# Output stage of an attention block on one Trainium2 core: scale, limit and old-stream add moved to VectorE in groups, column 0 and statistics at the end

## The chip, the cores and the metric

The kernel runs on one core of a Trainium2 chip. The metric is the device time of one execution in microseconds (us), from start to end of the program on the chip. The engines of the core that matter here are TensorE (PE in the profile, with its weight loads as PEld), VectorE (DVE), ScalarE (ACT), GpSimd (POOL) and SyncE (SP), which issues transfers (DMA). Each engine works through its own instructions in order; they meet at semaphores.

## The reference, cut to what matters

The program is two transformer layers on a stream of 4096 tokens by 256 columns. The part that the change touches is the end of the second layer's attention: the output projection, an exponential map at the point (1, 0, ..., 0), a limit, a new column 0, and the residual add; after it comes the layer norm of the mixture of experts.

```
def _project(x):
    sp = jnp.clip(x[..., 1:], -8.0, 8.0)
    x0 = jnp.sqrt(1.0 + jnp.sum(sp ** 2, axis=-1, keepdims=True) + EPS)
    return jnp.concatenate([x0, sp], axis=-1)
def _exp_map(x, v):
    vx = _inner(v, x)[..., None]
    v_tan = v + vx * x
    v_ns = jnp.maximum(_inner(v_tan, v_tan), 0.0)
    v_n = jnp.minimum(jnp.sqrt(v_ns + EPS)[..., None], 5.0)
    res = jnp.cosh(v_n) * x + jnp.sinh(v_n) * v_tan / (v_n + EPS)
    return _project(res)
...
    return _project(_exp_map(mu, out @ Wo.T))
...
x = x + _L1_attn_ref(_layernorm(x, axis=-1), ...)
x = x + _L1_ffn_ref(_layernorm(x, axis=-1), ...)
```

With mu = (1, 0, ..., 0) every token's columns 1 to 255 are multiplied by one number, sinh(v_n) / (v_n + EPS), and limited to -8 and 8; column 0 becomes the square root of 1 plus the sum of the 255 squares. Then the old stream is added, and mean and variance of each token are wanted.

## The kernel before, in words

The stream lies in the on-chip memory as `u` (the tile `wide_x` in the profile): 128 partitions, 32 token tiles `t` (NT) of 256 columns. The function `attention_out` is one stage, closed by a barrier of all engines. It runs in four phases, and each engine's order is the order in which the code is written.

1. Projection (L1792 to L1821 and L1867 to L1883). TensorE turns and multiplies, VectorE copies the product into `u` two tiles at a time, ScalarE squares each tile for v_n.
2. One small chain on tiles of 128x32 (L1824 to L1846), mostly on VectorE, with a square root and two exponentials on ScalarE. It ends in `g`, one factor for each token.
3. The loop over eight groups `n` of G = 4 tiles. ScalarE multiplies each tile by its column of `g` (`scale`, L1895), four instructions of 128x256 for a group, one group ahead. VectorE limits the group in one instruction of 128x1024 (L1851). ScalarE then squares each tile with an accumulated sum into `s2` (L1904); in the trace a square is an ACTIVATE and an ACTIVATION_READ_ACCUMULATOR.
4. When all 32 sums are there: VectorE adds 1 (L1853), ScalarE loads its table for the square root and takes it (L1907), VectorE writes column 0 (L1856), and then, group by group, adds the old stream `x2` (`ao_x`, 128x1024, L1861) and takes the statistics of the four tiles (`bn_stats`, L1864).

SyncE loads the old stream: groups 0 to 3 into a ring of four places at the start of the stage, then the weights of four experts (`meanwhile`, L1915 to L1918), then groups 4 to 7, each when the add of the group four before it is done. That wait is on the semaphore `added`, which the add on VectorE raises (L1861).

After the stage comes `route`: VectorE merges the statistics (`bn_aggr`, L323) and normalises the tiles (L335) for the router on TensorE and ScalarE. The first layer has a stage much like this one, `combine_and_log_map`, whose rows serve below: there VectorE normalises a tile with two per-partition operands (L1206), limits a group (L1209), and at the end multiplies tiles by one per-partition factor `lm_f` (L1236), while GpSimd adds pairs of rows (L1272).

Of the kernel before, what the change touches and what calls it, by code (L numbers as in the profile page):

```python
# [14 lines left out]
ALU = mybir.AluOpType  # L15
ACT = mybir.ActivationFunctionType
# [7 lines left out]
P = 128  # L24
T, C = 4096, 256
KC = C // P
NT = T // P
# [1731 lines left out]
def attention_out(nc, k, meanwhile):  # L1759
# [6 lines left out]
    G = 4  # L1766
    u = k.x
    NG, NPR, XR = NT // G, NT // 2, 4
    with Stage(nc, "ao") as s:
        x2 = s.sb("x2", [P, XR, G, C])  # L1770
        oT = s.sb("oT", [P, 2, KC, 2, P])
        junk = s.sb("junk", [P, C])
        s2, vn, e1, e2, t2, pl, sm, g = (s.sb(v, [P, NT]) for v in ("s2", "vn", "e1", "e2", "t2", "pl", "sm", "g"))
        psT = s.ps("psT", [P, 2, BANK])
        psU = s.ps("psU", [P, 3, 2 * C])
        (turned, oT_out, u_ready, u_out, squared, chain, asked, done_act, scaled, clipped, led, added) = (
# [3 lines left out]
        with nc.Block() as block:  # L1780
# [35 lines left out]
            @block.vector  # L1816
            def _(dve):
                ser = Serial(dve, chain)
                for n in range(NPR):
                    dve.wait_ge(u_ready, n + 1)  # L1820
                    dve.tensor_copy(u[:, 2 * n:2 * n + 2, :],  # L1821
                                    psU[:, n % 3, :].rearrange("p (t c) -> p t c", c=C)).then_inc(u_out, 1)
                dve.wait_ge(squared, NT)
                ser(dve.tensor_scalar(vn[:, :], s2[:, :], 0.0, EPS, ALU.max, ALU.add))  # L1824
                dve.sem_inc(asked, 1)
                dve.wait_ge(done_act, 1)
                ser(dve.tensor_scalar(vn[:, :], vn[:, :], 5.0, None, ALU.min))
                dve.sem_inc(asked, 1)

                ser(dve.tensor_tensor(t2[:, :], vn[:, :], vn[:, :], ALU.mult))  # L1830
                ser(dve.tensor_scalar(pl[:, :], t2[:, :], 1.0 / 42.0, 1.0, ALU.mult, ALU.add))
                ser(dve.scalar_tensor_tensor(pl[:, :], t2[:, :], 1.0 / 20.0, pl[:, :], ALU.mult, ALU.mult))
                ser(dve.tensor_scalar(pl[:, :], pl[:, :], 1.0, None, ALU.add))
                ser(dve.scalar_tensor_tensor(pl[:, :], t2[:, :], 1.0 / 6.0, pl[:, :], ALU.mult, ALU.mult))
                ser(dve.tensor_scalar(pl[:, :], pl[:, :], 1.0, None, ALU.add))
                ser(dve.tensor_tensor(pl[:, :], pl[:, :], vn[:, :], ALU.mult))
                ser(dve.tensor_scalar(sm[:, :], vn[:, :], 0.5, None, ALU.is_lt))
                dve.wait_ge(done_act, 3)
                ser(dve.tensor_tensor(e1[:, :], e1[:, :], e2[:, :], ALU.subtract))
                ser(dve.tensor_scalar(e1[:, :], e1[:, :], 0.5, None, ALU.mult))  # L1840
                ser(dve.tensor_tensor(pl[:, :], pl[:, :], e1[:, :], ALU.subtract))
                ser(dve.tensor_tensor(pl[:, :], pl[:, :], sm[:, :], ALU.mult))
                ser(dve.tensor_tensor(e1[:, :], e1[:, :], pl[:, :], ALU.add))
                ser(dve.tensor_scalar(t2[:, :], vn[:, :], EPS, None, ALU.add))
                ser(dve.reciprocal(e2[:, :], t2[:, :]))
                ser(dve.tensor_tensor(g[:, :], e1[:, :], e2[:, :], ALU.mult))  # L1846
                dve.sem_inc(asked, 1)
                for n in range(NG):
                    part = u[:, n * G:(n + 1) * G, :]
                    dve.wait_ge(scaled, (n + 1) * G)  # L1850
                    dve.tensor_scalar(part, part, -8.0, 8.0, ALU.max, ALU.min).then_inc(clipped, 1)  # L1851
                dve.wait_ge(squared, 2 * NT)
                ser(dve.tensor_scalar(s2[:, :], s2[:, :], 1.0, EPS, ALU.add, ALU.add))  # L1853
                dve.sem_inc(asked, 1)
                dve.wait_ge(done_act, 4)
                dve.tensor_copy(u[:, :, 0], s2[:, :]).then_inc(led, 1)  # L1856
                dve.wait_ge(led, 1)
                for n in range(NG):
                    part = u[:, n * G:(n + 1) * G, :]
                    dve.wait_ge(x2_in[n % XR], (n // XR + 1) * 16)  # L1860
                    dve.tensor_tensor(part, part, x2[:, n % XR, :, :], ALU.add).then_inc(added, 1)  # L1861
                    dve.wait_ge(added, n + 1)
                    for t in range(n * G, (n + 1) * G):
                        dve.bn_stats(k.st6[:, t, :], u[:, t, :])  # L1864

            @block.scalar
            def _(act):  # L1867
                for n in range(NPR + 1):
                    if n < NPR:
                        act.wait_ge(turned, n + 1)  # L1870
                        if n >= 2:

                            act.wait_ge(u_ready, n - 1)
                        act.activation(oT[:, n % 2, :, :, :].rearrange("p k q c -> p (k q c)"), psT[:, n % 2, :],
                                       ACT.Copy).then_inc(oT_out, 1)
                    if n:
                        m = n - 1
                        act.wait_ge(u_out, m + 1)
                        for q in range(2):
                            if m or q:  # L1880

                                act.wait_ge(squared, 2 * m + q)
                            act.activation(junk[:, 1:C], u[:, 2 * m + q, 1:C], ACT.Square,  # L1883
                                           accum_out=s2[:, 2 * m + q:2 * m + q + 1]).then_inc(squared, 1)
                act.wait_ge(asked, 1)
                act.activation(vn[:, :], vn[:, :], ACT.Sqrt).then_inc(done_act, 1)
                act.wait_ge(asked, 2)
                act.activation(e1[:, :], vn[:, :], ACT.Exp).then_inc(done_act, 1)
                act.activation(e2[:, :], vn[:, :], ACT.Exp, scale=-1.0).then_inc(done_act, 1)
                act.wait_ge(asked, 3)  # L1890
                act.wait_ge(u_out, NPR)

                def scale(n):
                    for t in range(n * G, (n + 1) * G):
                        act.activation(u[:, t, :], u[:, t, :], ACT.Copy, scale=g[:, t:t + 1]).then_inc(scaled, 1)  # L1895

                scale(0)
                for n in range(NG):
                    if n + 1 < NG:
                        scale(n + 1)  # L1900
                    act.wait_ge(clipped, n + 1)
                    for t in range(n * G, (n + 1) * G):
                        act.wait_ge(squared, NT + t)
                        act.activation(junk[:, 1:C], u[:, t, 1:C], ACT.Square,  # L1904
                                       accum_out=s2[:, t:t + 1]).then_inc(squared, 1)
                act.wait_ge(asked, 4)
                act.activation(s2[:, :], s2[:, :], ACT.Sqrt).then_inc(done_act, 1)  # L1907


# [290 lines left out]
```

## Time and profile before

| | |
|---|---|
| median of 3 runs | 2615.57 us (2615.17 to 2617.49) |
| the profiled execution: its own time | 2617.34 us |
| its span from first to last instruction | 2615.5 us |
| mean granted TensorE clock | 0.935 |
| VectorE busy | 1267.7 us (48%) |
| ScalarE busy | 1490.9 us (57%) |
| small chain ready (`g`) | 1849.25 us into the span |
| last statistics of the stage | 1900.98 us into the span |

The profiled execution is a run of its own, 1.8 us above the median. Busy shares are means over the whole program; the stage of the change is 2% of it, and what it costs is read from its own stretch, 1849 to 1902 us.

### The profile page before, as it was taken

The numbers are of one execution on the slowest core, as the hardware profiler recorded it, in microseconds if no ns is written. First come the engines' busy times: TensorE is split into PE (matmuls) and PEld (weight loads), VectorE is DVE, ScalarE is ACT, GpSimd is POOL, SyncE is SP. The second block draws the span as 40 slices with busy tenths as digits, with TensorE's granted clock in tenths as the row PEclk, the third lists the DMA queues.
The fourth block names the chain that finished last, engine by engine and source line by source line (L and its number), as shares of the span: only waits on it lengthen the run. The fifth ranks groups of instructions, "written<-read, shape, count | busy, mean of one in ns | idle before, by whom it ended". The sixth has DMA issues, their size and how long they took to land. (4 is left out here: it accounts for less than half of the span.)

```text
span 2615.5 us, 41239 instructions
## 1 busy us (share of the span) xinstructions
PE 2241.7 (86%) x12824; PEld 1058.3 (40%) x12825; DVE 1267.7 (48%) x2731; ACT 1490.9 (57%) x2463; POOL 383.2 (15%) x628
## 2 busy tenths in 40 slices
PE   4995799922978999999999999999157999999993
PEld 3783555511651222222222222224124666666662
DVE  5566422254885444444444444421465444444444
ACT  2212433213766999999999999997643222222220
POOL 0030366640000000000000000000001222222220
PEclk9998899965998999999999999999678999999996
DMA  5001122253100000000000000003353444434445
GB/s 179 1 1 65 33 79 78 74 187 124 36 14 1 1 1 1 1 1 1 1 1 1 1 1 1 1 1 102 93 169 103 122 121 118 120 118 118 120 116 210
DMA packets 106610, 164.39 MB, mean 63 GB/s; under 512 B 9592, under 2 KB 82032, under 8 KB 106480
## 3 DMA queue, kind: packets, MB, share of 16 engines
q1 hardware_dynamic: 91696, 121.24, 15.1%
q0 software_dynamic: 13632, 37.24, 4.3%
q10 hardware_dynamic: 1152, 4.19, 0.4%
q8 instruction: 79, 1.29, 0.2%
q14 instruction: 51, 0.42, 0.0%
HBM read 123.06 MB, written 39.58 MB: 62 GB/s over the span
## 5 line engine op out<-in xcount | busy, mean ns | idle before, releaser
L1661 ACT ACTIVATE at_pexp<-at_psS 128x1024 f32<-128x1024 f32 x1024 | 968.1, 1023 | 59.9 <-PE at_psS L1561 56.9
L1675 DVE TENSOR_REDUCE at_mx<-at_psM 128x1 f32<-128x512 f32 x474 | 327.5, 691 | 478.4 <-PE at_psM L1588 478.4
L1575 PE MATMUL at_psO<-at_pexp,at_vst 128*32 128x512 f32 x4096 | 546.5, 606 | 0.1
L1561 PE MATMUL at_psS<-l1c_QT,l1c_KT 64*128 64x512 f16 x2048 | 404.3, 387 | 12.2 <-ACT at_pexp L1661 6.1
L1561 PEld LDWEIGHTS at_psS<-l1c_QT,l1c_KT 64*128 64x128 f16 x2048 | 100.7, 93 | 616.7 <-ACT at_pexp L1661 555.7
L1988 PE MATMUL ex_psH<-wide_wgu,ex_xT 128*128 x852 | 339.7, 549 | 0.1
L2032 ACT ACTIVATE ex_sg<-ex_bias 128x228 f32<-128x228 f32 x213 | 83.7, 393 | 287.9 <-DVE ex_bias L2058 287.9
L2058 DVE TENSOR_TENSOR ex_bias<-ex_psH,ex_bias 128x456 f32<-128x456 f32 x213 | 134.7, 633 | 198.5 <-PE ex_psH L1988 197.3
L1988 PEld LDWEIGHTS ex_psH<-wide_wgu,ex_xT 128*128 128x128 f32 x852 | 157.4, 191 | 138.1 <-issue 138.0
L1005 POOL DMA_INDIRECT expert_rows<-ex_y,ex_odx x142 | 140.4, 989 | 397.8 <-issue 281.4
L2011 PE MATMUL ex_psY<-wide_w2b,ex_hT 114*128 (+1 forms) x852 | 196.0, 380 | 0.7 <-DVE ex_y L2077 0.7
L1588 PE MATMUL at_psM<-at_ksumT,l1c_QT 64*128 64x512 bf16 x474 | 179.2, 378 | 0.6
L2011 PEld LDWEIGHTS ex_psY<-wide_w2b,ex_hT 114*128 114x128 f32 (+1 forms) x852 | 156.5, 190 | 19.6 <-issue 1.3
L999 POOL DMA_INDIRECT ex_xg<-normed,ex_idx x142 | 139.6, 983 | 112.0 <-POOL ex_odx L990 97.6
L1055 PE MATMUL ex_psH<-l_w,ex_xT 128*128 x284 | 141.9, 623 | 5.3 <-issue 1.1
L1537 POOL COPY at_vst<-wide_x 128x512 f32<-128x512 f32 x16 | 9.7, 608 | 898.7 <-PE at_psO L1575 898.6
L1575 PEld LDWEIGHTS at_psO<-at_pexp,at_vst 128*32 128x32 f32 x4096 | 80.9, 108 | 130.1 <-issue 121.6
L266 PE MATMUL w_ps<-top_ident,w_raw 128*128 128x128 f32 x128 | 23.3, 333 | 116.3 <-DMA w_raw<-in_L_attn_Wq 90.6
L1116 DVE TENSOR_SCALAR ex_y<-ex_psY,top_wgt 128x256 f32<-128x256 f32 x71 | 34.3, 484 | 176.8 <-DMA expert_rows<-ex_y,ex_odx 94.9
L2024 ACT ACTIVATE ex_xT<-ex_psX 128x256 f32<-128x256 f32 x71 | 27.2, 383 | 157.5 <-PE ex_psX L1977 157.5
L1093 ACT ACTIVATE ex_hT<-ex_psG 128x256 f32<-128x256 f32 x71 | 27.2, 383 | 132.1 <-PE ex_psG L1064 132.1
L985 POOL CAST ex_idx<-top_tok 128x1 uint32 (+1 forms) x142 | 28.6, 201 | 427.4 <-POOLq L74 304.1
(335 smaller groups left out, 2696.0 us busy)
## 6 DMA issues: line engine op xcount, KB each, us to landing
ex_bias<-in_L_ffn_bg SPq DMA_DIRECT2D x71, 342.0 KB, 4.7
ex_bias<-in_L_ffn_b SPq DMA_DIRECT2D x71, 342.0 KB, 5.1
normed<-rt_area SPq DMA_DIRECT2D x16, 512.0 KB, 2.6
lm_y<-expert_rows SPq DMA_DIRECT2D x16, 512.0 KB
cb_y<-expert_rows SPq DMA_DIRECT2D x16, 512.0 KB, 9.6
w_raw<-in_L_ffn_w SPq DMA_DIRECT2D x24, 256.0 KB, 4.2
wide_wgu<-in_L_ffn_Wg SPq DMA_DIRECT2D x8, 684.0 KB
wide_wgu<-in_L_ffn_W SPq DMA_DIRECT2D x8, 684.0 KB
```

The costliest lines, as they stand in the source:

```text
L999: pool.indirect_dma_start(xg[:, g, :], None, k.xn_d, bass.IndirectOffsetOnAxis(idx[:, g, :], 0)).then_inc(got[g], 16)
L1005: pool.indirect_dma_start(k.y_d, bass.IndirectOffsetOnAxis(odx[:, j, :], 0), y[:, j, :], None).then_inc(put[j], 16)
L1055: mm = pe.matmul(psH[:, j, :], xT[:, j, kk, :], k.w13[:, ds(e, 1), kk, :].rearrange("p a c -> p (a c)"), start=(kk == 0), stop=(kk == KC - 1))
L1561: mm = pe.matmul(psS[:, n, hh * BANK:(hh + 1) * BANK], keys(k.KT, p)[r, kt * P:(kt + 1) * P], keys(k.QT, p)[r, c * BANK:(c + 1) * BANK], s ...
L1575: mm = pe.matmul(psO[g * VW:(g + 1) * VW, y, :], vst[:, p % 2, hh, kt, :], pexp[:, (p * ST + step) % 3 * 2 + n, hh * BANK:(hh + 1) * BANK] ...
L1588: pe.matmul(psM[:, :], keys(k.QT, p)[r, t * P:(t + 1) * P], ksumT[r, p % 2, :], start=True, stop=True).then_inc(maxed, 1)
L1661: act.activation(pexp[:, u % 6, :], psS[:, u % 2, :], ACT.Exp, scale=D ** -0.5 / (QS * QS)).then_inc(raised, 1)
L1675: dve.tensor_reduce(mx[:, n:n + 1], psM[:, :], AX.X, ALU.max).then_inc(reduced, 1)
L1988: mm = pe.matmul(psH[:, n, 0:G2].rearrange("p (n c) -> p n c", n=2), xT[:, j, kk, :], k.wgu[:, ds(e, 1), kk, :, n * HW:(n + 1) * HW].rearr ...
L2011: mm = pe.matmul(psY[:, 0:C], hT[0:rows, j, g, :], k.w2b[0:rows, ds(e, 1), g, :].rearrange("p a c -> p (a c)"), start=(g == 0), stop=(g == ...
L2032: act.activation(sg[:, n, :], bias[:, st.slot(1, BR), n, 0, :], ACT.Silu).then_inc(gated, 1)
L2058: dve.tensor_tensor(hb, psH[:, n, 0:G2].rearrange("p (n c) -> p n c", n=2), hb, ALU.add).then_inc(added, 1)
```

## The change

VectorE takes over the multiplication by `g`, which also does the lower limit (L1852 of the changed kernel); the group's instruction of 128x1024 does the upper limit alone (L1855). The add of the old stream for columns 1 to 255 moves into the same loop, one group behind (L1862), and a copy of the old stream's column 0 goes to a small tile `x0` first (L1860), because the ring place is given back by the add. ScalarE keeps only the squares. Column 0 is written once, as root plus `x0` (L1868), after the last add, and the 32 statistics follow it in one run (L1871).

```
+        x0 = s.sb("x0", [P, NT])
...
-                dve.sem_inc(asked, 1)
-                for n in range(NG):
-                    part = u[:, n * G:(n + 1) * G, :]
-                    dve.wait_ge(scaled, (n + 1) * G)
-                    dve.tensor_scalar(part, part, -8.0, 8.0, ALU.max, ALU.min).then_inc(clipped, 1)
+                for n in range(NG + 1):
+                    if n < NG:
+                        part = u[:, n * G:(n + 1) * G, :]
+                        for t in range(n * G, (n + 1) * G):
+                            dve.tensor_scalar(u[:, t, :], u[:, t, :], g[:, t:t + 1], -8.0, ALU.mult,
+                                              ALU.max).then_inc(scaled, 1)
+                        dve.wait_ge(scaled, (n + 1) * G)
+                        dve.tensor_scalar(part, part, 8.0, None, ALU.min).then_inc(clipped, 1)
+                    if n:
+                        m = n - 1
+                        part = u[:, m * G:(m + 1) * G, 1:C]
+                        dve.wait_ge(x2_in[m % XR], (m // XR + 1) * 16)
+                        dve.tensor_copy(x0[:, m * G:(m + 1) * G], x2[:, m % XR, :, 0])
+                        dve.wait_ge(squared, NT + (m + 1) * G)
+                        dve.tensor_tensor(part, part, x2[:, m % XR, :, 1:C], ALU.add).then_inc(added, 1)
                 dve.wait_ge(squared, 2 * NT)
                 ser(dve.tensor_scalar(s2[:, :], s2[:, :], 1.0, EPS, ALU.add, ALU.add))
                 dve.sem_inc(asked, 1)
                 dve.wait_ge(done_act, 4)
-                dve.tensor_copy(u[:, :, 0], s2[:, :]).then_inc(led, 1)
+                dve.wait_ge(added, NG)
+                dve.tensor_tensor(u[:, :, 0], s2[:, :], x0[:, :], ALU.add).then_inc(led, 1)
                 dve.wait_ge(led, 1)
-                for n in range(NG):
-                    part = u[:, n * G:(n + 1) * G, :]
-                    dve.wait_ge(x2_in[n % XR], (n // XR + 1) * 16)
-                    dve.tensor_tensor(part, part, x2[:, n % XR, :, :], ALU.add).then_inc(added, 1)
-                    dve.wait_ge(added, n + 1)
-                    for t in range(n * G, (n + 1) * G):
-                        dve.bn_stats(k.st6[:, t, :], u[:, t, :])
+                for t in range(NT):
+                    dve.bn_stats(k.st6[:, t, :], u[:, t, :])
...
-                act.wait_ge(asked, 3)
-                act.wait_ge(u_out, NPR)
-
-                def scale(n):
-                    for t in range(n * G, (n + 1) * G):
-                        act.activation(u[:, t, :], u[:, t, :], ACT.Copy, scale=g[:, t:t + 1]).then_inc(scaled, 1)
-
-                scale(0)
                 for n in range(NG):
-                    if n + 1 < NG:
-                        scale(n + 1)
                     act.wait_ge(clipped, n + 1)
                     for t in range(n * G, (n + 1) * G):
                         act.wait_ge(squared, NT + t)
                         act.activation(junk[:, 1:C], u[:, t, 1:C], ACT.Square,
                                        accum_out=s2[:, t:t + 1]).then_inc(squared, 1)
-                act.wait_ge(asked, 4)
+                act.wait_ge(asked, 3)
                 act.activation(s2[:, :], s2[:, :], ACT.Sqrt).then_inc(done_act, 1)
```

VectorE from the end of the small chain (`ao_g` is `g`, `ao_s` is `s2`, `top_st` the statistics), before the change: all eight limits, then the tail, of which the first two groups stand here.

```order
L1846 TENSOR_TENSOR ao_g<-ao_e 128x32
L1851 TENSOR_SCALAR wide_x<-wide_x 128x1024 x8
L1853 TENSOR_SCALAR ao_s<-ao_s 128x32
L1856 COPY wide_x<-ao_s 128x32
L1861 TENSOR_TENSOR wide_x<-wide_x,ao_x 128x1024
L1864 BN_STATS top_st<-wide_x 128x6 x4
L1861 TENSOR_TENSOR wide_x<-wide_x,ao_x 128x1024
```

The same place after the change, up to the limit of group 2 (the copy L1860 reads the old stream and writes `x0`, and both are named `ao_x` there).

```order
L1847 TENSOR_TENSOR ao_g<-ao_e 128x32
L1852 TENSOR_SCALAR wide_x<-wide_x,ao_g 128x256 x4
L1855 TENSOR_SCALAR wide_x<-wide_x 128x1024
L1852 TENSOR_SCALAR wide_x<-wide_x,ao_g 128x256 x4
L1855 TENSOR_SCALAR wide_x<-wide_x 128x1024
L1860 COPY ao_x<-ao_x 128x4
L1862 TENSOR_TENSOR wide_x<-wide_x,ao_x 128x4x255
L1852 TENSOR_SCALAR wide_x<-wide_x,ao_g 128x256 x4
L1855 TENSOR_SCALAR wide_x<-wide_x 128x1024
```

Each group's four multiplications stand ahead of its limit, and the add of a group stands behind the limit of the next one. The end of the stage on VectorE after the change:

```order
L1855 TENSOR_SCALAR wide_x<-wide_x 128x1024
L1860 COPY ao_x<-ao_x 128x4
L1862 TENSOR_TENSOR wide_x<-wide_x,ao_x 128x4x255
L1860 COPY ao_x<-ao_x 128x4
L1862 TENSOR_TENSOR wide_x<-wide_x,ao_x 128x4x255
L1864 TENSOR_SCALAR ao_s<-ao_s 128x32
L1868 TENSOR_TENSOR wide_x<-ao_s,ao_x 128x32
L1871 BN_STATS top_st<-wide_x 128x6 x32
```

No add of the old stream is left behind the root; only the 32 statistics are. ScalarE before the change, from the exponentials on:

```order
L1888 ACTIVATE ao_e<-ao_vn 128x32
L1889 ACTIVATE ao_e<-ao_vn 128x32
L1895 ACTIVATE wide_x<-wide_x,ao_g 128x256 x8
L1904 ACTIVATE ao_junk,ao_s<-wide_x 128x255 x4
L1895 ACTIVATE wide_x<-wide_x,ao_g 128x256 x4
```

And ScalarE after the change, from the same place to the end of the stage:

```order
L1895 ACTIVATE ao_e<-ao_vn 128x32
L1896 ACTIVATE ao_e<-ao_vn 128x32
L1901 ACTIVATE ao_junk,ao_s<-wide_x 128x255 x32
L1904 ACT_TABLE_LOAD
L1904 ACTIVATE ao_s<-ao_s 128x32
```

The 32 multiplications are gone from ScalarE, no table load has come between the exponentials and the squares, and the one for the square root stands directly behind the last square, as before.

## Rows read from the trace of the kernel before

**Rows 1.** The page: busy time, share of the span and instructions of each engine
```profile
PE 2241.7 (86%) x12824; PEld 1058.3 (40%) x12825; DVE 1267.7 (48%) x2731; ACT 1490.9 (57%) x2463; POOL 383.2 (15%) x628
```
**Rows 2.** Busy time by stretch (busy us and instructions of each engine; TensorE clock; DMA share)
```profile
1849.30:1878.50 29.20, 0.00 (x0) 0.00 (x0) 5.55 (x8) 28.31 (x96) 0.00 (x0) 0.50 0.06 21
1878.50:1901.00 22.50, 0.00 (x0) 0.00 (x0) 20.73 (x42) 1.55 (x3) 0.00 (x0) 0.50 0.32 94
```
**Rows 3.** Who waited for whom, 1843 to 1925 us: us in total, times, longest
```profile
PE rt_psT L790 <- DVE rt_area L335: 63.5, 1, 63.5
DVE wide_x L1851 <- ACT wide_x L1895: 20.2, 8, 2.9
DVE top_mv L323 <- PEq L74: 0.8, 1, 0.8
```
**Rows 4.** Timeline of ScalarE, the group loop: start, us, what
```profile
1849.34 3.30 ACT L1895 ACTIVATE wide_x<-wide_x,ao_g 128x256 f32<-128x256 f32 x8 [2.47 <-DVEq L1847]
...
1854.57 1.69 ACT L1895 ACTIVATE wide_x<-wide_x,ao_g 128x256 f32<-128x256 f32 x4
1856.16 0.40 ACT L1904 ACTIVATE ao_junk<-wide_x 128x255 f32<-128x255 f32 x1
...
1858.08 0.19 ACT L1904 ACTIVATION_READ_ACCUMULATOR ao_junk<-wide_x 128x1 f32 x1
1858.18 1.69 ACT L1895 ACTIVATE wide_x<-wide_x,ao_g 128x256 f32<-128x256 f32 x4
...
1878.35 0.19 ACT L1904 ACTIVATION_READ_ACCUMULATOR ao_junk<-wide_x 128x1 f32 x1
1878.56 1.28 ACT L1907 ACT_TABLE_LOAD   x1
1879.85 0.23 ACT L1907 ACTIVATE ao_s<-ao_s 128x32 f32<-128x32 f32 x1
```
**Rows 5.** Timeline of VectorE, from `g` to the barrier
```profile
1849.06 0.19 DVE L1846 TENSOR_TENSOR ao_g<-ao_e 128x32 f32<-128x32 f32 x1
...
1878.57 0.18 DVE L1853 TENSOR_SCALAR ao_s<-ao_s 128x32 f32<-128x32 f32 x1 [3.54 <-ACT ao_junk L1904]
1880.11 0.20 DVE L1856 COPY wide_x<-ao_s 128x32 f32<-128x32 f32 x1 [1.36 <-ACT ao_s L1907]
1880.35 1.23 DVE L1861 TENSOR_TENSOR wide_x<-wide_x,ao_x 128x1024 f32<-128x1024 f32 x1
1881.61 1.40 DVE L1864 BATCH_NORM_STATS2 top_st<-wide_x 128x6 f32<-128x256 f32 x4
1882.93 1.21 DVE L1861 TENSOR_TENSOR wide_x<-wide_x,ao_x 128x1024 f32<-128x1024 f32 x1
...
1899.57 1.41 DVE L1864 BATCH_NORM_STATS2 top_st<-wide_x 128x6 f32<-128x256 f32 x4
```
**Rows 6.** VectorE's groups by form: busy us, mean ns of one, idle before
```profile
L1861 DVE TENSOR_TENSOR wide_x<-wide_x,ao_x 128x1024 f32<-128x1024 f32 x8 | 9.7, 1210 | 0.0
L1851 DVE TENSOR_SCALAR wide_x<-wide_x 128x1024 f32<-128x1024 f32 x8 | 5.6, 694 | 20.2 <-ACT wide_x L1895 20.2
L1236 DVE TENSOR_SCALAR lm_sp<-lm_sp,lm_f 128x256 f32<-128x256 f32 x16 | 4.3, 346 | 0.1
L2167 DVE TENSOR_SCALAR l1w_wqkv<-l1w_wqkv 128x1024 f32<-128x1024 f32 x1 | 0.7, 695 | 0.9 <-PEq L74 0.9
L877 DVE TENSOR_SCALAR rt_mask<-rt_one 128x256 f32<-128x256 f32 x2 | 0.6, 294 | 0.1
```
**Rows 7.** Timeline of VectorE in the first layer's like stage
```profile
566.53 2.35 DVE L1199 TENSOR_SCALAR lm_std<-top_mv 128x4 f32<-128x4 f32 x1
...
615.62 4.29 DVE L1236 TENSOR_SCALAR lm_sp<-lm_sp,lm_f 128x256 f32<-128x256 f32 x16
```
**Rows 8.** GpSimd at that first place, and the spread of L1199
```profile
566.51 2.34 POOL L1272 TENSOR_TENSOR lm_y<-lm_y 128x1024 f32<-128x1024 f32 x1 [3.07 <-DMA lm_y<-expert_rows]
...
L1199 DVE TENSOR_SCALAR lm_std<-top_mv x8: 169/446/2352, 560.9 to 603.8; 128x4 f32<-128x4 f32 x8
```
**Rows 9.** Loads of the old stream: landing, and the last four on SyncE
```profile
DMA to landing us min/median/max: 3.5/3.7/7.3
...
1881.60 8.01 SPq L1790 DMA_DIRECT2D ao_x<-stream  x4
```
**Rows 10.** Busy time by stretch, around the end of the weight loads (columns as rows 2)
```profile
1852.00:1854.00 2.00, 0.00 (x0) 0.00 (x0) 0.69 (x1) 1.94 (x8) 0.00 (x0) 0.50 0.35 116
1854.00:1856.00 2.00, 0.00 (x0) 0.00 (x0) 0.00 (x0) 1.97 (x8) 0.00 (x0) 0.50 0.02 7
```

## The prediction

> **What bounds the kernel now.** The page's busy shares come first: TensorE leads with 86% [rows 1], but that is a mean over a program of many stages, so they only say that no engine has an answer for this one. The page's chain covers the last 35 us alone. So I read the stage by stretches of time. From 1849.3 to 1878.5 us ScalarE is busy 28.31 of 29.20 us and VectorE 5.55; from 1878.5 to 1901 VectorE is busy 20.73 of 22.50 and ScalarE 1.55; TensorE and GpSimd do nothing in either [rows 2]. Two engines thus work one after the other. The waits say the same: VectorE's eight limits wait 20.2 us for ScalarE's multiplications, and TensorE's next work waits 63.5 us, ended by VectorE's first normalised tile [rows 3]. Everything after the stage hangs on VectorE's last statistics, so a microsecond off the path from `g` to there should be a microsecond off the program.
>
> The timeline of ScalarE shows its price for a group: four multiplications and four squares, 3.61 us from one group to the next (1854.57 to 1858.18) [rows 4]; 32 multiplications and 32 squares make 1849.34 to 1878.54. That of VectorE shows the tail: from 1880.35 to 1900.98, eight times 2.57 us for an add and four statistics [rows 5].
>
> **The change, part by part.** I lay the new instructions out in time from rows, and measure the new end against the old one, 1900.98.
>
> *Prices.* A multiplication by a per-partition factor on a tile of 128x256 in on-chip memory is L1236: 346 ns for one [rows 6], and 16 in a row take 4.29 us [rows 7], so the next starts (4.29 - 0.346) / 15 = 0.263 us after the one before. The new one adds a constant lower limit to it. With constants alone that shape takes 294 ns [rows 6], and a limit with two constants on 128x1024 takes 694, so a second operation is not what costs. Four: 3 x 0.263 + 0.346 = 1.14 us. The upper limit is an instruction of the old form: 0.69, and 0.04 before it, since it waits for the four (gaps of this kind, 0.03 to 0.04, stand between an instruction and one that waits for it, as from 1880.31 to 1880.35 [rows 5]). An instruction behind one that it does not wait for starts 0.08 before that one's end (1881.61 + 1.40 is 1883.01, the next starts at 1882.93 [rows 5]). The copy of 128x4 has no row: the nearest, L1199, has the same size and takes 0.17 at the least and 2.35 beside GpSimd [rows 7, 8]. GpSimd is idle here, so I take 0.17, overlapped at both ends, 0.08 of the path, and keep 0.17 as its upper bound. The add on 4x255 columns reads 1020 elements instead of 1024: 1.21 [rows 6].
>
> *A group on VectorE:* 1.14 + 0.04 + 0.69 - 0.08 + 0.08 + 1.21 - 0.08 = 3.00 us. *A group on ScalarE:* the squares alone, 1856.16 to 1858.27, 2.11 us [rows 4]. So the pace passes from ScalarE (3.61) to VectorE (3.00), and ScalarE waits 0.9 us in each group.
>
> *In time.* `g` is there at 1849.25 [rows 5]. Group 0 is multiplied 1849.29 to 1850.43 and limited by 1851.16; group 1 is limited by 1852.95. ScalarE squares group 0 from 1851.19 to 1853.30, so the first add waits 0.4 us and ends at 1854.54. This is the one place where the add waits for squares: from then on an add starts 3.00 us behind its group's limit and the squares need 2.14. Group 2 starts at 1854.46, group 7 five periods later at 1869.46, limited by 1871.33. Its squares end at 1873.47, while VectorE is through with the add of group 6 at 1872.54 and waits 0.96 us. The last add runs 1873.50 to 1874.71.
>
> *The tail.* ScalarE's table load needs no semaphore: it stood 0.02 us behind the last square before [rows 4], so it runs 1873.47 to 1874.75, under the last add, and about 1.3 us of it leave the path. `s2` plus 1 ends at 1874.81, the root (0.23) at 1875.07, column 0 (0.20) at 1875.30. The statistics start at 1875.34. Four take 1.40 where one takes 0.41 (L1864 spaced 0.33), so 32 take 31 x 0.33 + 0.41 = 10.6 us: the end is 1885.95, 15.0 us before the old one. By parts: 29.2 us of loop become 24.2, and 22.4 us behind the last square become 12.5, and the difference there is the eight adds, 1.24 each with its gap: seven now lie under the squares, and the last lies over the table load, in whose place it stands.
>
> The table load is where a page is weighed. The row has 1.28 us of load and the root 0.01 behind it, so the root waits for 1.28 only [rows 4]. The Trainium skill, page "ScalarE: Activation LUTs", section "What ACT_TABLE_LOAD costs", says that a switch costs about 2.66 us, the load and a drain of 1.38 with it. By that estimate the root would end 1.3 us later and the gain be 13.7; the trace does not agree with it, and the sum goes by the row.
>
> *What is moved past queues.* SyncE's loads of groups 4 to 7 wait for the adds. They were issued from 1881.60 [rows 9] and now could be from 1854.6, one each 3 us. The weight loads ahead of them have drained: the transfer share is 0.35 up to 1854 and 0.02 after [rows 10]. The load for group 4 has from 1854.6 to 1865.3, 10.8 us, and the slowest of the eight landed in 7.3 [rows 9]: hidden. If that cover went, each us of landing beyond 10.8 would be a us on the path. Behind the add on VectorE the next group's multiplications are queued, and ScalarE's squares wait for those. The barrier's 0.8 us [rows 3] stays.
>
> *Sum.* The profiled execution took 2617.34 us with a span of 2615.5; less 15.0 it would be 2602.3. The median of the runs shown is 1.8 us lower, and there the same 15.0 gives 2600.6, which is my forecast.
>
> **Rivals.**
> *A. The multiplications run at one element per cycle.* 346 ns for 256 columns and 694 for 1024 fit a rate of two per cycle; at one, 1024 elements take 1210 [rows 6]. The new instruction mixes a per-partition factor and a constant in two operations, a mix that no row has. At half the rate each costs 0.13 more, a group 0.54; the 0.4 us wait takes up part of the first, so the gain is 11.0: 2604.6. Against it: neither a factor (L1236) nor two constants (L1851) alone lose the rate. Chance 9%.
> *B. VectorE is slowed by ScalarE at its side; slower than before.* L1199 is a 4-element instruction that took 2.35 us beside a GpSimd instruction of 2.34, and 0.17 when clear [rows 7, 8]: an instruction of this kind can be held by another engine. If ScalarE's squares did so, each of the six one-source instructions of a group (four multiplications, limit, copy) could wait up to one square, 0.54 us: 3.2 us a group, 26 in all, and the kernel takes 11 us more, about 2627. It decides from a period of 5.0 us upwards (15 us over 7.4 periods, since the first group counts in part), and is slower by 0.2% from 5.8. Against it: L1851 takes 694 ns with ScalarE at work beside it and L2167, the same form behind a barrier, 695 [rows 6]. Chance 2%.
> The Trainium skill, page "VectorE: DVE Perf Modes", section "Two Vector instructions with no wait between them", calls the second read interface shared with GpSimd and names no other engine; by that rule B would cost nothing here, since GpSimd is idle.
> *C. The old stream is late.* If landing took 20 us, the gain would be 15.0 - 9.2 = 5.8, about 2609.8; slower than before from 25.8. The slowest of eight took 7.3 [rows 9]. Chance 2%.
> *D. The gain is given back,* with the end of the stage 15 us earlier and the program as long as before, 2615.6. For it there would have to be something that comes at a fixed time; the only transfers from before the stage, the weights, end by 1854 [rows 10]. Chance 3%.
>
> **How the numbers follow.** The forecast has 84%. Its own range: the copy at 0.17 takes 0.7 us off the gain; multiplications spaced by their full 346 ns another 2.0; nothing for copy and first wait adds 1.0; the medians themselves spread 1 us either way. That is 2598.3 to 2604.3. Taking in A, I give 2598.3 to 2605.5. A measurement of this kernel tells about 0.2%, 5.2 us, from no change: the forecast, A and C are faster by more (95%, rounded down to 94), D is within it (3, with some of B 4), B beyond it (2).
>
> **What the profile after would show.** L1852 at about 346 ns, groups 3.0 us apart, so group 7's limit near 1871.3; the first add with a short wait for ScalarE, the last with about 1 us, none between. The table load under the last add, column 0 near 1875, statistics in one run of 10.6 us to about 1886. L1852 near 480 ns means A; L1855 above 0.7 beside squares means B; adds of groups 4 to 7 waiting for a transfer mean C; an end near 1886 with the old total means D. What makes the prediction wrong is above all the price of L1852 and the overlaps, since each counts 7 or 31 times.

## The result, and the profile after

The changed kernel took 2600.89 us (median of 4 runs, 2600.41 to 2602.46) against 2615.88 for the kernel before beside it (4 runs, 2615.17 to 2617.49): a ratio of 0.9944 [0.9929, 0.9959] (in brackets, here and below, a 95% interval). The forecast was 2600.6.

The profiled execution took 2600.85 us with a span of 2598.9. Busy shares of the page, which answer to [rows 1]:

```profile
PE 2240.3 (86%) x12824; PEld 1055.4 (41%) x12825; DVE 1274.2 (49%) x2771; ACT 1479.3 (57%) x2431; POOL 382.8 (15%) x628
```

They hardly moved, as they hardly would for 15 us in 2600: VectorE has 40 instructions more and ScalarE 32 fewer. The stage shows in pieces of time, with the columns of [rows 2]. Their bounds are those of the predicted schedule; the stage began 1.7 us earlier in this execution, so the second piece also takes in the first microsecond of `route`:

```profile
1849.30:1873.50 24.20, 0.00 (x0) 0.00 (x0) 22.36 (x54) 17.78 (x66) 0.00 (x0) 0.50 0.38 113
1873.50:1886.00 12.50, 0.00 (x0) 0.00 (x0) 11.67 (x48) 0.00 (x0) 0.00 (x0) 0.50 0.00 0
```

VectorE, the third busy column, now works through both pieces, and ScalarE beside it in the first. Before, one of the two was mostly idle in each. The waits from 1843 to 1910 us:

```profile
PE rt_psT L790 <- DVE rt_area L335: 48.4, 1, 48.4
...
ACT ao_junk L1901 <- DVE wide_x L1855: 9.4, 7, 4.3
...
DVE wide_x L1862 <- ACT ao_junk L1901: 1.3, 2, 0.9
...
DVE top_mv L323 <- PEq L74: 0.8, 1, 0.8
...
DVE wide_x L1868 <- ACT ao_s L1904: 0.4, 1, 0.4
```

The 20.2 us that VectorE spent waiting for ScalarE's multiplications [rows 3] are gone, ScalarE waits for VectorE instead, and TensorE's wait, which spans the stage, is 48.4 us where it was 63.5: 15.1 less. VectorE's timeline, the answer to [rows 5]:

```profile
1847.36 0.19 DVE L1847 TENSOR_TENSOR ao_g<-ao_e 128x32 f32<-128x32 f32 x1
1847.59 1.14 DVE L1852 TENSOR_SCALAR wide_x<-wide_x,ao_g 128x256 f32<-128x256 f32 x4
...
1851.65 1.22 DVE L1862 TENSOR_TENSOR wide_x<-wide_x,ao_x 128x1020 f32<-128x1020 f32 x1 [0.34 <-ACT ao_junk L1901]
1852.79 1.14 DVE L1852 TENSOR_SCALAR wide_x<-wide_x,ao_g 128x256 f32<-128x256 f32 x4
1853.96 0.69 DVE L1855 TENSOR_SCALAR wide_x<-wide_x 128x1024 f32<-128x1024 f32 x1
1854.57 0.16 DVE L1860 COPY ao_x<-ao_x 128x4 f32<-128x4 f32 x1
1854.64 1.21 DVE L1862 TENSOR_TENSOR wide_x<-wide_x,ao_x 128x1020 f32<-128x1020 f32 x1
1855.77 1.13 DVE L1852 TENSOR_SCALAR wide_x<-wide_x,ao_g 128x256 f32<-128x256 f32 x4
...
1871.74 1.22 DVE L1862 TENSOR_TENSOR wide_x<-wide_x,ao_x 128x1020 f32<-128x1020 f32 x1 [0.91 <-ACT ao_junk L1901]
1872.88 0.17 DVE L1864 TENSOR_SCALAR ao_s<-ao_s 128x32 f32<-128x32 f32 x1
1873.41 0.21 DVE L1868 TENSOR_TENSOR wide_x<-ao_s,ao_x 128x32 f32<-128x32 f32 x1 [0.35 <-ACT ao_s L1904]
1873.65 10.55 DVE L1871 BATCH_NORM_STATS2 top_st<-wide_x 128x6 f32<-128x256 f32 x32
```

A group comes 2.98 us after the one before (1852.79 to 1855.77). Only the first and the last add wait for squares. The new instruction's price, in VectorE's groups by form from 1849 to 1887 (four of the 32 lie ahead of it):

```profile
L1852 DVE TENSOR_SCALAR wide_x<-wide_x,ao_g 128x256 f32<-128x256 f32 x28 | 7.9, 346 | 0.0
L1855 DVE TENSOR_SCALAR wide_x<-wide_x 128x1024 f32<-128x1024 f32 x8 | 5.6, 694 | 0.3
```

ScalarE's timeline at the end of the squares, which answers to [rows 4]:

```profile
1871.52 0.19 ACT L1901 ACTIVATION_READ_ACCUMULATOR ao_junk<-wide_x 128x1 f32 x1
1871.73 1.28 ACT L1904 ACT_TABLE_LOAD   x1
1873.15 0.23 ACT L1904 ACTIVATE ao_s<-ao_s 128x32 f32<-128x32 f32 x1
```

**Where the 15 us lie.** I call the time from the end of `g` to the end of the last statistics *the stretch*; it is what the change touches, and it is read the same way in every run below. Before it was 1849.25 to 1900.98, 51.73 us; after, 1847.55 to 1884.20, 36.65: 15.08 less (predicted: 36.70, 15.0). The loop, to the end of the last square, takes 24.16 of it and the rest 12.49 (predicted: 24.2 and 12.5). The two profiled executions are 16.49 us apart (2617.34 and 2600.85). The rest is 1.70, by which `g` was ready sooner in that execution, ahead of anything changed, and -0.29 after the stage and around the span. The medians are 15.0 apart; their interval alone would allow 10.7 to 18.6, so it is the stretch that confirms the size.

### The profile page after: what moved, and what is told of

The parts are those of the page before. It is cut to its first block and busy times, and to the rows that moved or that the text cites. A ratio compares the mean times of both kernels' runs of the same rounds, so it can differ in the third digit from the quotient of the medians.

```text
span 2598.9 us, 41245 instructions
## 1 busy us (share of the span) xinstructions
PE 2240.3 (86%) x12824; PEld 1055.4 (41%) x12825; DVE 1274.2 (49%) x2771; ACT 1479.3 (57%) x2431; POOL 382.8 (15%) x628
```

## Experiments

All are edits of the changed kernel. Each was run beside the kernel before, and ratios are to it; only the last three had the changed kernel beside them, so small differences are read from the stretch. Medians of the kernel before: 2617.87 for the runs on one part, the multiply alone and GpSimd; 2617.09 for late loads, root by group, one scale and both; 2617.28 for the last three.

**One part alone: new split, adds where they were.** VectorE scales and limits, but the adds follow all squares again, each with its four statistics.

```diff
+                for n in range(NG):
...
+                    dve.tensor_scalar(part, part, 8.0, None, ALU.min).then_inc(clipped, 1)
...
-                        dve.tensor_tensor(part, part, x2[:, m % XR, :, 1:C], ALU.add).then_inc(added, 1)
...
+                    dve.tensor_tensor(part, part, x2[:, n % XR, :, :], ALU.add).then_inc(added, 1)
```

> The adds of the old stream and column 0 go back behind the root, as before the change; VectorE keeps the multiplications. Theory (the pace passes to whichever engine has most to do in a group): VectorE needs 1.14 + 0.04 + 0.69 - 0.08 = 1.79 us a group, ScalarE's squares 2.17 with their handover, so ScalarE sets the pace; squares from 1851.2 to 1868.5 us with the small chain ready at 1849.25, then the old tail of 22.4 us to 1890.9: 10.1 us less than the kernel before, about 2605.8, and 4.9 more than the changed kernel. Rival (the two parts of the change add up: the loop went from 29.2 to 24.2 us for the multiplications, the tail from 22.4 to 12.5 for the adds): 5 us less than before, about 2611.

Measured: 2607.95 us, ratio 0.9961 [0.9947, 0.9976]; the stretch is 1849.41 to 1891.45, 42.04. Its timeline of VectorE:

```profile
1861.30 0.69 DVE L1853 TENSOR_SCALAR wide_x<-wide_x 128x1024 f32<-128x1024 f32 x1
1861.91 1.14 DVE L1850 TENSOR_SCALAR wide_x<-wide_x,ao_g 128x256 f32<-128x256 f32 x4
1863.08 0.69 DVE L1853 TENSOR_SCALAR wide_x<-wide_x 128x1024 f32<-128x1024 f32 x1
1869.05 0.18 DVE L1855 TENSOR_SCALAR ao_s<-ao_s 128x32 f32<-128x32 f32 x1 [5.28 <-ACT ao_junk L1896]
```

VectorE is through every 1.78 us and then waits 5.28: now ScalarE's squares set the pace. This part alone brings 9.69 us of stretch (10.1 were expected; the rival had 5).

**The other part alone: adds in the loop, ScalarE scales.**

```diff
-                            dve.tensor_scalar(u[:, t, :], u[:, t, :], g[:, t:t + 1], -8.0, ALU.mult,
...
+                        dve.tensor_scalar(part, part, -8.0, 8.0, ALU.max, ALU.min).then_inc(clipped, 1)
...
+                        act.activation(u[:, t, :], u[:, t, :], ACT.Copy, scale=g[:, t:t + 1]).then_inc(scaled, 1)
```

> The multiplications stay on ScalarE as before the change, a group ahead, with both limits in VectorE's one instruction; the adds stay in the loop, a group behind, and the statistics in one run at the end. Theory: ScalarE keeps its 3.61 us a group, VectorE's 0.69 + 0.08 + 1.21 lie beside it; squares end 29.3 us after the small chain as before, the last add lies over the table load, and the tail is 12.5 us: 9.9 us less than before, about 2606.0. Rival (without the multiplications moved the adds collide with ScalarE's work and stretch it, or cost the loop their own time): a group takes 3.61 + 1.21, the gain is eaten, about 2616. Together with the run that puts the adds last: if each alone gives 10 and both together 15, the parts overlap by 5.

Measured: 2608.65 us, ratio 0.9968 [0.9954, 0.9982]; the stretch is 1847.87 to 1889.67, 41.80. Timeline of VectorE:

```profile
1853.31 1.22 DVE L1860 TENSOR_TENSOR wide_x<-wide_x,ao_x 128x1020 f32<-128x1020 f32 x1 [1.25 <-ACT ao_junk L1909]
1854.91 0.69 DVE L1853 TENSOR_SCALAR wide_x<-wide_x 128x1024 f32<-128x1024 f32 x1 [0.38 <-ACT wide_x L1900]
...
1856.92 1.22 DVE L1860 TENSOR_TENSOR wide_x<-wide_x,ao_x 128x1020 f32<-128x1020 f32 x1 [1.25 <-ACT ao_junk L1909]
```

ScalarE's old pace of 3.61 us stands, VectorE waits for it twice in each group, and the adds fill its idle time. This part alone brings 9.93 us. The two gains sum to 19.6, both together bring 15.1: with the new split VectorE idles only 5.28 us under the squares and the eight adds need 9.7, so the rest of them, 4.4 us, is back on the path. The rival, a group of 3.61 + 1.21 us, did not come.

**Is the second operation free?** The lower limit goes back to the limit's own instruction.

```diff
-                            dve.tensor_scalar(u[:, t, :], u[:, t, :], g[:, t:t + 1], -8.0, ALU.mult,
-                                              ALU.max).then_inc(scaled, 1)
+                            dve.tensor_scalar(u[:, t, :], u[:, t, :], g[:, t:t + 1], None,
+                                              ALU.mult).then_inc(scaled, 1)
...
+                        dve.tensor_scalar(part, part, -8.0, 8.0, ALU.max, ALU.min).then_inc(clipped, 1)
```

> The multiplication has no limit in it any more, and the wide instruction does both limits. Theory (a second operation of a one-source instruction is free, and the mix of a per-partition factor and a constant does not lose the rate of two elements per cycle): 346 ns for the multiplication, 694 for the wide one, 3.0 us a group, the time of the changed kernel within 0.5 us. Rival (each operation costs time): 4 x 0.05 us a group less in the first and as much more in the second; a multiplication below 330 ns or a wide one above 720 would show it.

Measured: 2601.52 us, ratio 0.9937 [0.992, 0.9953]; the stretch is 1850.41 to 1887.06, 36.65, the same to the hundredth. VectorE's groups by form:

```profile
L1852 DVE TENSOR_SCALAR wide_x<-wide_x,ao_g 128x256 f32<-128x256 f32 x32 | 9.1, 346 | 0.0
L1855 DVE TENSOR_SCALAR wide_x<-wide_x 128x1024 f32<-128x1024 f32 x8 | 5.6, 694 | 0.3
```

346 and 694 ns with one operation or two. Which instruction holds the lower limit doesn't matter.

**The adds on GpSimd.** They move to an idle engine. Each waits for its group's squares and for VectorE's copy of the old column 0 (`kept`); VectorE waits for none of them inside the loop.

```diff
+            @block.gpsimd
...
+                    pool.wait_ge(kept, m + 1)
+                    pool.tensor_tensor(part, part, x2[:, m % XR, :, 1:C], ALU.add).then_inc(added, 1)
...
-                        dve.tensor_tensor(part, part, x2[:, m % XR, :, 1:C], ALU.add).then_inc(added, 1)
```

> GpSimd does the eight adds of 4x255 columns in the loop; VectorE keeps multiplication, limit and the copy of column 0. Theory (GpSimd's work holds VectorE's one-source instructions, as 2.35 us for a 4-element instruction beside a GpSimd add of 2.34 showed in the first layer): VectorE's group is 1.79 us plus most of 2.34, about 4.1, and the last add is 1.1 us longer: 8 us or more above the changed kernel, about 2610. Rival (the engines run side by side): VectorE 1.79, ScalarE 2.17, GpSimd 2.4 a group, so GpSimd sets the pace and the loop ends 2 us earlier than in the changed kernel: about 2599.

Measured: 2609.76 us, ratio 0.997 [0.9959, 0.9982]; the stretch is 1848.74 to 1892.12, 43.38. Timelines of VectorE and of GpSimd:

```profile
1850.56 1.14 DVE L1862 TENSOR_SCALAR wide_x<-wide_x,ao_g 128x256 f32<-128x256 f32 x4
...
1856.35 3.28 DVE L1862 TENSOR_SCALAR wide_x<-wide_x,ao_g 128x256 f32<-128x256 f32 x4
...
1881.33 0.21 DVE L1875 TENSOR_TENSOR wide_x<-ao_s,ao_x 128x32 f32<-128x32 f32 x1 [2.36 <-POOL wide_x L1801]
```
```profile
1856.61 2.34 POOL L1801 TENSOR_TENSOR wide_x<-wide_x,ao_x 128x1020 f32<-128x1020 f32 x1 [1.13 <-DVE ao_x L1869]
1860.60 2.34 POOL L1801 TENSOR_TENSOR wide_x<-wide_x,ao_x 128x1020 f32<-128x1020 f32 x1 [1.65 <-DVE ao_x L1869]
```

The same four multiplications take 1.14 us with GpSimd idle and 3.28 beside an add of 2.34: they stand still for 2.14 of it. The add is off VectorE, but not out of its time, and a group takes 3.99 us (1856.61 to 1860.60). At the end VectorE waits 2.36 us more for the last add. The stretch is 6.73 us above the changed kernel's; I had expected 8 or more, so the mechanism was right and its price too high. The median came out at the expected 2610 with a kernel before that was 2 us slower here, which is luck.

**Take away the loads' cover.** SyncE issues the loads of groups 4 to 7 three adds later (for group 4 after the fourth add, not the first), so that each has less time ahead of its use.

```diff
-                        sp.wait_ge(added, n - XR + 1)
+                        sp.wait_ge(added, n)
```

> SyncE's loads of groups 4 to 7 each wait for three more adds than in the changed kernel, so each is issued only when the add directly in front of it is done. Theory (the loads are hidden because group 4's has 10.8 us from the first add; with three adds more it has 1.8, and every later one 1.8 too): each of the four adds waits for its load, landing 3.6 to 7.2 us less 1.8, so 8 to 20 us more than the changed kernel in four pieces, about 2609 to 2620, which is the price of the cover if it goes. Rival (some other slack, or a load that lands much sooner than the trace says): no wait before the adds of groups 4 to 7, time as the changed kernel.

Measured: 2612.29 us (10 runs, 2608.44 to 2615.0), ratio 0.9983 [0.9973, 0.9993]; the stretch is 1848.31 to 1894.08, 45.77, so 9.1 more. Timeline of VectorE, and for the line of the loads, who waited for it:

```profile
1866.45 0.17 DVE L1860 COPY ao_x<-ao_x 128x4 f32<-128x4 f32 x1 [2.10 <-DMA ao_x<-stream]
1866.53 1.21 DVE L1862 TENSOR_TENSOR wide_x<-wide_x,ao_x 128x1020 f32<-128x1020 f32 x1
```
```profile
  DVE ao_x L1860: 9.8, 4
...
DMA to landing us min/median/max: 3.6/3.8/7.3
```

With the cover gone, the copy that opens each add waits for the transfer: four waits, 9.8 us, almost all of it on the path. The expected cover of 1.8 us holds for three of them (1.86 to 2.10 us of wait); group 7 has none, because no multiplications stand between its copy and the add before it, and waits 3.72:

```profile
1881.55 0.17 DVE L1860 COPY ao_x<-ao_x 128x4 f32<-128x4 f32 x1 [3.72 <-DMA ao_x<-stream]
```

This is the mechanism of rival C, here by less cover and not by a slower landing; the landing itself is as before [rows 9].

**What is left, 1: the root by group.** The loop takes the root of each group's sums and writes its column 0, so the statistics can begin in the last add's wait, and the tail of `s2`, root and column goes. The square-root table is loaded ahead of the loop.

```diff
+                act.activation(junk[:, 0:1], one[:, 0:1], ACT.Sqrt)
...
+                    act.activation(s2[:, at], s2[:, at], ACT.Sqrt, bias=one[:, 0:1]).then_inc(done_act, 1)
...
+                    dve.tensor_tensor(u[:, at, 0], s2[:, at], x0[:, at], ALU.add).then_inc(led, 1)
```

> ScalarE takes the root group by group, its table loaded once ahead of the loop while it is idle; VectorE writes column 0 group by group, one behind, and does the statistics of group 0 while it would wait for the last squares. Theory (VectorE is the bound; what is left on its path besides work is 0.9 us before the last add, and 0.6 for the root and s2): a group costs 0.08 more for the small add, the waits go, from the small chain to the last statistics 35.7 us where the changed kernel has 36.65. Rival (the small root in ScalarE's queue and the extra waits stretch the loop): a group above 3.15 us, no gain.

Measured: 2600.9 us, ratio 0.9938 [0.9921, 0.9955]; the stretch is 1847.45 to 1883.13, 35.68: 0.97 less than in the changed kernel, as expected. Timeline of VectorE, where the first statistics now stand in front of the last add, which waits for nothing:

```profile
1871.27 1.40 DVE L1859 BATCH_NORM_STATS2 top_st<-wide_x 128x6 f32<-128x256 f32 x4
1872.58 1.20 DVE L1879 TENSOR_TENSOR wide_x<-wide_x,ao_x 128x1020 f32<-128x1020 f32 x1
```

**What is left, 2: one of four multiplications back on ScalarE,** which waits in each group. Both limits go to the wide instruction, as in the run with the multiply alone, where that cost nothing.

```diff
-                        for t in range(n * G, (n + 1) * G):
+                        for t in range(n * G, (n + 1) * G - 1):
...
+                    act.activation(u[:, t, :], u[:, t, :], ACT.Copy, scale=g[:, t:t + 1]).then_inc(scaled_act, 1)
```

> Of a group's four multiplications ScalarE takes one, a group ahead, VectorE three. Theory (the busier engine sets the pace): VectorE 2.98 - 0.26 = 2.72 us a group, ScalarE 2.17 + 0.40 = 2.57, so 2.72; from the small chain to the last statistics about 34.9 us instead of 36.65, the total 1.8 us below the changed kernel. Rival (the exchange between the engines costs more than 0.26 us a group): a group at 3.0 or above, no gain.

Measured: 2600.11 us, ratio 0.9935 [0.9918, 0.9951]; the stretch is 1849.81 to 1884.74, 34.93: 1.72 less than in the changed kernel, as expected, with groups 2.72 us apart:

```profile
1856.49 1.21 DVE L1865 TENSOR_TENSOR wide_x<-wide_x,ao_x 128x1020 f32<-128x1020 f32 x1
...
1859.21 1.21 DVE L1865 TENSOR_TENSOR wide_x<-wide_x,ao_x 128x1020 f32<-128x1020 f32 x1
```

The expected 1.8 us in the total can't be told from these runs.

**Both.**

> Both: the root by group, and one of four multiplications on ScalarE. Theory: VectorE 2.80 us a group, ScalarE 2.17 + 0.40 + about 0.3 for the root = 2.9, so ScalarE sets the pace again at about 2.9, and the stretch from the small chain to the last statistics is 34.5 to 35.3 us; the gains of the two (1.0 and 1.8) do not add up. Rival (they add up, the root is hidden on ScalarE): 33.9 us.

Measured: 2599.65 us, ratio 0.9937 [0.992, 0.9953]; the stretch is 1845.64 to 1879.60, 33.96. The rival was right and my theory wrong: the two gains add up (36.65 less 0.97 less 1.72 is 33.96). Timeline of ScalarE:

```profile
1852.33 0.30 ACT L1931 ACTIVATE ao_s<-ao_s,ao_one 128x4 f32<-128x4 f32 x1
1852.54 0.49 ACT L1918 ACTIVATE wide_x<-wide_x,ao_g 128x256 f32<-128x256 f32 x1
```

The root lasts 0.30 but takes only 0.21 from one start to the next, so ScalarE needs 2.75 us a group (root to root, 1852.33 to 1855.08), less than the 2.79 of VectorE. I had put the root at its full 0.3 us and so had the pace pass to ScalarE.

**Both, with the root written in place.** The root goes straight to column 0 and the add runs over all 256 columns, without the copy and the small add; groups 4 and 7 keep their fourth multiplication on VectorE.

```diff
-                        dve.tensor_tensor(part, part, x2[:, m % XR, :, 1:C], ALU.add).then_inc(added, 1)
+                        dve.tensor_tensor(part, part, x2[:, m % XR, :, :], ALU.add).then_inc(added, 1)
...
+                    act.activation(u[:, at, 0], s2[:, at], ACT.Sqrt, bias=one[:, 0:1]).then_inc(done_act, 1)
```

> ScalarE writes each group's root into column 0 of the stream, VectorE's add then takes all 256 columns, so the copy of the old column 0 and the small add of column 0 are gone; of the eight groups two (4 and 7) have all four multiplications on VectorE. Theory (both engines near 2.75 us a group, 0.15 less on VectorE, moved so that neither leads): from the small chain to the last statistics about 33.4 us, 3.2 us below the changed kernel. Rival (the add now waits for the root as well, which stands behind four squares, and ScalarE sets the pace): adds that wait in the middle of the loop, and 34 us or more.

Measured: 2600.85 us, ratio 0.9936 [0.9922, 0.9949]; the stretch is 1845.95 to 1880.07, 34.12. Timeline of VectorE:

```profile
1850.31 1.23 DVE L1873 TENSOR_TENSOR wide_x<-wide_x,ao_x 128x1024 f32<-128x1024 f32 x1 [1.08 <-ACT wide_x L1921]
```

The rival was right here too. The add now waits for the root, so the first stands 1.08 us where it stood 0.60 in the kernel with both. From the first add to that of group 6 the two kernels take the same (16.77 and 16.75 us): the two small instructions less give back 0.15 us a group, the two multiplications that VectorE took back cost 0.26 each, and adds that start only behind their root (at 1853.06, 0.01 after the limit's end, where an add that waits for nothing starts 0.08 before it) take the rest.

**The changed kernel and the one with both, five runs each on one chip.**

> The changed kernel once more, beside the two versions built on it, so that the three are compared on one chip. Theory: 15.1 us below the kernel before, 0.9942 of it, whatever this chip's level is. Rival (part of the 16.5 us between the two profiled executions came from the stage): the stretch from the small chain to the last statistics is other than 36.65 us in this profile.

> Root by group and one multiplication of four on ScalarE, once more, with more rounds. Theory (what leaves the stretch leaves the program): 33.96 us for the stretch again, and the total 2.7 us below the changed kernel, a ratio to the kernel before of about 0.9932; the rounds may be too few to tell 0.1%. Rival (given back later): the stretch shorter, the rest of the program longer by as much.

Measured: 2599.18 us (2598.56 to 2604.82), 0.9936 [0.9922, 0.9949], and 2599.05 (2598.66 to 2602.71), 0.9935 [0.9921, 0.9948]. The stretches are 36.66 and 33.99. The changed kernel is 18.1 us below the kernel before here, where 15.1 were expected; the interval, 13.3 to 20.4 us below, holds both, and the stretch is as before, so nothing says that the stage gave more. The two medians are 0.1 us apart with 2.7 us less in the stretch, and the runs of the one kernel spread over 6.3 us and those of the other over 4.0: no version tried beats the changed kernel by more than its runs can tell, and the runs can't tell either whether the 2.7 us reached the total. In the two profiled executions (2601.22 and 2598.66 us) the total differs by 2.56: 1.34 of it because `g` was ready sooner, 2.67 in the stretch, and about 1.4 lost again behind it. What of that shows in the next stage stands below.

## Why the prediction was right

It was right in the sum and in its terms: every mark of the laid-out schedule, counted from `g`, came within 0.1 us. **The price of L1852:** 346 ns was taken from L1236 with a second operation at nothing; 346 was measured, and with the second operation taken out again still 346. Rival A, half the rate, is refuted. **The group on VectorE:** 3.00 predicted, 2.98 measured; the copy lasts 0.16 and the add starts 0.07 behind the copy's start. **Nothing held up by ScalarE:** four multiplications took 1.14 us with ScalarE idle (the first, at 1847.59) and 1.13 beside squares (at 1855.77), the limit 694 ns as before. Rival B is refuted as far as ScalarE goes; the engine that does hold VectorE is GpSimd, as [rows 7, 8] had it for one instruction and the adds on GpSimd for a whole loop. The Trainium skill, page "VectorE: DVE Perf Modes", section "Two Vector instructions with no wait between them", names GpSimd alone as sharing VectorE's second read interface; these two runs agree (1.13 beside ScalarE, 3.28 beside GpSimd).

**The waits:** 0.4 at the first add, 0.96 at the last, none between; 0.34, 0.91 and none were measured. **The table load under the last add:** it began 0.02 behind the last square, and the root started 1.42 us after it, 0.10 behind `s2` (1872.88 + 0.17), so `s2` released it and not the load. The hand-over from `s2` to the root was put at 0.03. The Trainium skill, page "ScalarE: Activation LUTs", section "What ACT_TABLE_LOAD costs", has 2.66 us for a switch; by that estimate the root would have started at 1874.39. It started at 1873.15, so the trace does not agree. **The tail:** 10.6 predicted for the statistics, 10.55 measured. **The loads:** they landed in 7.2 us at most, the last four in 3.6, and nobody waited for them. Rival C needed less cover, which the late loads gave it, and then a us of waiting was nearly a us on the path (9.8 and 9.1), as it had said. **Rival D,** the gain given back: the stretch and the medians fell by 15.1 and 15.0, so it did not happen to the change. Whether it happened to the last 2.7 us, those of both edits on top, is not shown: in the one pair of profiled executions about 1.4 of them came back behind the stage. **The range:** its own terms put the low end at 2598.6 (1.0 for copy and first wait, 1.0 for the medians), not 2598.3; nothing hangs on it here.

The prediction parted the gain by time, 5.0 us in the loop and 9.9 behind it, and not by edit. The runs give it by edit: the new split alone brings 9.7 us and the early adds alone 9.9, and of these 4.5 overlap. So neither edit owns a fixed share of the 15.

## What to carry to other kernels

When two engines work one after the other on the same tiles, lay both engines' instructions for one group side by side from rows of the same form: the longer of the two sums is the new period, and the first and last group, where one still waits for the other, are counted by themselves. Two such edits fill the same idle time, so their gains need not add, and each engine's sum is written down again for the two together: 9.7 and 9.9 made 15.1, while the later 0.97 and 1.72 did add, because VectorE's sum stayed the longer. Do not move work to an idle GpSimd on the strength of its idleness: here an add there held VectorE's multiplications for nine tenths of its length.

## What the runs showed of the hardware

**An add on GpSimd holds VectorE's one-source instructions, squares on ScalarE don't.** The numbers stand above: 2.14 us of a 2.34 us add, against 1.13 us for four multiplications beside squares. The hold ended with the add: in the same run an instruction of 128x32 that began at 1878.53, when an add had begun at 1876.58, took 0.43 us instead of 0.17, so it was through at 1878.96, 0.04 behind that add's 2.34 us, though GpSimd went on with the next. All these instructions read one tensor; VectorE's own adds, which read two, never stood beside a GpSimd add in this stage.

**The clock behind the idle stretch was not the same in all executions.** TensorE idles through this stage at a granted clock of 0.50, the lower of its two levels (1.2 of 2.4 GHz), and then has 16 transposes and the router's matmuls. The piece from 6 to 12 us behind the first L323 (that is the first instruction of `route` on VectorE), in the changed kernel of the last runs, the one with both beside it, and the one with one scale (columns as [rows 2], TensorE's clock third from the end):

```profile
1890.77:1896.77 6.00, 6.00 (x22) 1.99 (x21) 3.27 (x8) 6.00 (x28) 0.00 (x0) 0.86 0.51 208
```
```profile
1886.76:1892.76 6.00, 5.99 (x20) 2.01 (x20) 3.27 (x8) 5.48 (x24) 0.00 (x0) 0.72 0.55 226
```
```profile
1891.55:1897.55 6.00, 5.70 (x22) 1.87 (x21) 3.26 (x8) 6.00 (x28) 0.00 (x0) 0.97 0.53 217
```

The same work gets 0.72 to 0.97. It is not set by the kernel alone: the changed kernel had 0.95 in its first profiled execution and 0.86 in this one. TensorE's timelines of the first two show the price: the same four matmuls behind the same 16 take 1.99 us in one and 2.82 in the other. The granted clock was 0.50 in both through the 16, and 0.93 and 0.66 on average over the four.

```profile
1888.35 3.92 PE L790 MATMUL rt_psT<-top_ident,rt_area 128*128 128x128 f32 x16 [48.44 <-DVE rt_area L335]
1892.20 1.99 PE L800 MATMUL rt_psLT<-rt_area,top_cent 128*8 128x512 f32 x4
```
```profile
1884.35 3.92 PE L790 MATMUL rt_psT<-top_ident,rt_area 128*128 128x128 f32 x16 [45.77 <-DVE rt_area L335]
1888.20 2.82 PE L800 MATMUL rt_psLT<-rt_area,top_cent 128*8 128x512 f32 x4
```

From the first L323 to the end of the span it is 713.73 us before, 713.90 and 714.53 in the two executions of the changed kernel, 714.14 with the multiply alone and 713.75 with one scale (clock in that piece 0.95, 0.95, 0.86, 0.95 and 0.97), and 715.57 to 716.45 with the root by group, with both in either run, with the root in place and with either part alone (0.70 to 0.79). That goes together, but not everywhere: the late loads had 0.73 and still needed only 714.03, and the adds on GpSimd had 0.94 and needed 715.06.

Between the changed kernel of the last runs and the one with both beside it the difference is 1.41 us, and 0.73 of it is there when TensorE begins its second four of these matmuls (6.89 us behind the first transpose in one, 7.62 in the other). So the clock behind an idle stretch is a part of what a small edit ahead of it gains or loses; where the other half goes stays open. It also stays open what decides how soon the clock comes back: the moment at which the stage ends is one candidate, and no run here varied it alone.

And `g` was ready anywhere from 1845.6 to 1850.4 us in the profiled executions, though hardly an instruction ahead of it was changed. For both reasons the time between two marks, which came out within 0.03 us when a kernel was profiled twice (36.65 and 36.66; 33.96 and 33.99), told of the small edits what totals could not.
